# One pair of PSUM banks for the running sum, two pairs for the state, in a chunked selective-scan block

## The reference, cut to what matters

```python
def step(h, inp):                     # one chunk of 128 tokens
    x_c, d_c, B_c, C_c = inp
    A_bar = jnp.exp(d_c[..., None] * A)
    BX = d_c[..., None] * B_c[:, :, None, :] * x_c[..., None]
    log_A_cum = jnp.cumsum(jnp.log(jnp.maximum(A_bar, EPS)), axis=1)
    A_cum = jnp.exp(jnp.minimum(log_A_cum, LOG_CLAMP))
    A_cum_sh = jnp.concatenate([jnp.ones_like(A_cum[:, :1]), A_cum[:, :-1]], axis=1)
    wcum = jnp.cumsum(BX / jnp.maximum(A_cum_sh, EPS), axis=1)
    h_chunk = A_cum * wcum / jnp.maximum(A_bar, EPS) + h[:, None] * A_cum
    y_c = jnp.einsum('bls,blds->bld', C_c, h_chunk) + D_param * x_c
    return (h_chunk[:, -1], y_c)
```

## Time and profile before

| | |
|---|---|
| time, median of 3 runs | 5796.58 us (5792.49 to 5797.22) |
| the profiled execution: its own time / its span | 5795.46 us / 5793.5 us |
| mean granted TensorE clock | 0.992 of full speed |
| PE busy | 5611.7 us (97%) |
| DVE busy | 5350.9 us (92%) |
| ACT busy | 3733.7 us (64%) |
| POOL busy | 2456.2 us (42%) |

### The profile page before, as it was taken

The page is one execution under the profiler, slowest core; times in us unless marked ns, Lnnn a source line. Parts: engine busy times, 40 slices in busy tenths (PEclk is TensorE's granted clock), DMA queues, the critical chain, the costliest instruction groups (busy, mean ns, idle before and its releaser), DMA issues. The chain is left out here.

```text
span 5793.5 us, 78230 instructions
## 1 busy us (share of the span) xinstructions
PE 5611.7 (97%) x16088; PEld 2641.4 (46%) x16152; DVE 5350.9 (92%) x7057; ACT 3733.7 (64%) x4615; POOL 2456.2 (42%) x2139
## 2 busy tenths in 40 slices
PE   8999999999999999999999999999999999999997
PEld 3444444444444444444444444444444444444443
DVE  7999999999999999999999999999999999999997
ACT  5666666666666666666666666666666666666664
POOL 3444444444444444444444444444444444444443
PEclk9999999999999999999999999999999999999999
DMA  2212212112121121121211212212112121121220
GB/s 69 19 16 16 20 14 18 16 15 20 14 18 18 16 18 16 15 20 14 18 17 15 20 14 17 20 14 18 16 15 20 14 18 17 17 18 16 15 18 12
DMA packets 158421, 104.23 MB, mean 18 GB/s; under 512 B 121024, under 2 KB 121024, under 8 KB 158016
## 3 DMA queue, kind: packets, MB, share of 16 engines
q1 hardware_dynamic: 158016, 100.71, 19.0%
HBM read 42.63 MB, written 16.78 MB: 10 GB/s over the span
## 5 line engine op out<-in xcount | busy, mean ns | idle before, releaser
L496 POOL TENSOR_SCALAR room<-total,limit 128x1024 f32<-128x1024 f32 x1024 | 1182.9, 1155 | 3244.6 <-PE cum L1068 475.1
L754 ACT ACTIVATE decay<-cum,neg_a 128x1024 f32<-128x1024 f32 x1024 | 1137.4, 1111 | 1539.2 <-PE cum L1068 1535.4
L1078 PE MATMUL state<-sources,tri_upto 128*128 128x512 f32 x4096 | 1971.8, 604 | 124.4 <-DVE term L1415 124.0
L1068 PE MATMUL cum<-step,tri_before 128*128 128x512 f32 x4096 | 1937.4, 595 | 0.1
L1415 DVE SCALAR_TENSOR_TENSOR term<-state,crow,decay 128x1024 f32<-128x1024 f32 x1024 | 1312.8, 1282 | 313.4 <-PE state L1078 197.1
L1425 DVE TENSOR_TENSOR acc<-acc,term 128x1024 f32<-128x1024 f32 x1024 | 1362.3, 1330 | 0.2
L1402 DVE SCALAR_TENSOR_TENSOR sources<-cum,brow,dx 128x1024 f32<-128x1024 f32 x1024 | 1305.8, 1275 | 7.2 <-ACT cum L770 7.2
L1068 PEld LDWEIGHTS cum<-step,tri_before 128*128 128x128 f32 x4096 | 780.1, 192 | 963.9 <-issue 939.2
L770 ACT ACTIVATE cum<-room,pos_a 128x1024 f32<-128x1024 f32 x1024 | 1143.5, 1117 | 108.9 <-POOL room L496 100.1
L1078 PEld LDWEIGHTS state<-sources,tri_upto 128*128 128x128 f32 x4096 | 742.5, 190 | 995.5 <-issue 867.8
L485 POOL TENSOR_SCALAR step<-delta,limit 128x1024 f32<-128x1024 f32 x1024 | 1144.5, 1118 | 42.7 <-DVE delta L1317 42.7
(11 more groups left out here) (127 smaller groups left out, 3626.3 us busy)
## 6 DMA issues: line engine op xcount, KB each, us to landing
hfirst<-hrows SPq DMA_DIRECT2D x496, 64.0 KB, 3.9
xt<-in_x SPq DMA_DIRECT2D x64, 256.0 KB, 2.6
hrows<-term SPq DMA_DIRECT2D x1024, 4.0 KB, 1.7
xres<-in_x SPq DMA_DIRECT2D x64, 256.0 KB, 2.6
out_x<-xres SPq DMA_DIRECT2D x64, 256.0 KB, 2.1
gate_last<-gate SPq DMA_DIRECT2D x512, 0.5 KB, 2.1
hrows<-hrows SPq DMA_DIRECT2D x64, 64.0 KB, 2.3
win<-in_w_in SPq DMA_DIRECT2D x2, 1024.0 KB, 7.9
```

What stands on the lines that cost most here:

```text
L496: nc.gpsimd.tensor_scalar(room[:, :], total[:, :], limit[:, s:s + 1], 0.0, ALU.min, ALU.max).then_inc(limited, 1)
L754: nc.scalar.activation(decay[s % 4][:, :], cum[s % 2][:, :], ACT.Exp, scale=neg_a[:, s:s + 1]).then_inc(decay_ready, 1)
L1068: last = nc.tensor.matmul(cum[s % 2][:, cols], tri_before[:, :], step[s % 2][:, cols], start=True, stop=True)
L1078: last = nc.tensor.matmul(state[:, cols], tri_upto[:, :], source[s % 2][:, cols], start=True, stop=True)
```

## The change

PSUM is dealt out anew: one pair of banks for `cum`, two pairs for `state`. `growths` writes its result into the `state` pair of the same slot instead of into `cum`; `states(s)` then overwrites it after `source(s)` has read it. With that, `states(s)` no longer waits for `term(s-1)`; `growths(s)` waits for `term(s-2)`, and `cumulate(s)` waits for `decays(s-1)`. `room` gets two buffers. The orders within slot s become:

- TensorE: `states(s)`, extras(s), `cumulate(s+2)`.
- ScalarE: some extras, `decays(s+1)`, `growths(s+1)`, the other extras.
- VectorE: `term(s-1)`, `add(s-1)`, extras(s), `source(s+1)`.
- GpSimd: `turn(s)`, `limit_step(s+2)`, `limit_sum(s+2)`.

Room for the second `room` buffer in SBUF comes from letting three small tiles share others (`ones` in `xnT[1]`, `csel` in `xi`, `qT` in `q_bf`). ScalarE's code path for `room` is removed; it had been used by no slot. The diff, cut to its core:

```diff
-        room = sb("room", [P, DI])
+        room = [sb(f"room{i}", [P, DI]) for i in range(2)]
...
+        qT = q_bf[:, :].rearrange("p (k t) -> p k t", t=P)
...
-        cum = [ps(f"cum{i}", [P, DI]) for i in range(2)]
-        state = ps("state", [P, DI])
+        cum = ps("cum", [P, DI])
+        state = [ps(f"state{i}", [P, DI]) for i in range(2)]
+        growth = state
...
             def limit_sum(t, s):
-                user, old = before(t, s, 1)
+                user, old = before(t, s, 2)
                 if user is not None:
                     pool.wait_ge(growth_ready, slot_at(user, old))
...
             def turn(t, s, more, more2):
...
                 else:
-                    pool.wait_ge(source_ready, slot_at(t, s))
+                    pool.wait_ge(added, slot_at(t, s - 2))
             def body(t, more, more2):                      # GpSimd
                 for s in range(NS):
                     turn(t, s, more, more2)
-                    if s + 2 < NS and s + 2 in ROOM_POOL:
+                    if s + 2 < NS:
+                        limit_step(t, s + 2)
                         limit_sum(t, s + 2)
...
-                    if s + 3 < NS:
-                        limit_step(t, s + 3)
...
             def end_q(t):                                  # ScalarE
...
+                if t.shift(-1) is not None:
+                    act.wait_ge(end_pe, at(END_PE, t.shift(-1), "ffn"))
                 nc.scalar.activation(q_bf[:, :], xn2, ACT.Identity, bias=round_back).then_inc(end_act, 1)
...
             def growths(t, s):
-                act.wait_ge(decay_ready, slot_at(t, s))
+                user, old = before(t, s, 2)
+                if user is not None:
+                    act.wait_ge(term_ready, slot_at(user, old))
+                act.wait_ge(limited, slot_at(t, s))
+                nc.scalar.activation(growth[s % 2][:, :], room[s % 2][:, :], ACT.Exp, scale=pos_a[:, s:s + 1]).then_inc(growth_ready, 1)
...
             def body(t, more, more2):                      # ScalarE
                 for s in range(NS):
-                    ahead, slot = (t, s + 2) if s + 2 < NS else (nxt, s + 2 - NS)
+                    ahead, slot = (t, s + 1) if s + 1 < NS else (nxt, 0)
...
                         decays(ahead, slot)
                     if s == 0 and prev is not None:
                         finish(prev)
+                    if more or s + 1 < NS:
+                        growths(ahead, slot)
                     if more:
                         if s == 0:
                             front_xi(nxt, 0)
...
-                    if more or s + 2 < NS:
-                        growths(ahead, slot)
...
             def cumulate(t, s):                            # TensorE
-                user, old = before(t, s, 2)
+                user, old = before(t, s, 1)
                 if user is not None:
-                    pe.wait_ge(source_ready, slot_at(user, old))
+                    pe.wait_ge(decay_ready, slot_at(user, old))
...
             def states(t, s):
                 pe.wait_ge(source_ready, slot_at(t, s))
-                user, old = before(t, s, 1)
-                if user is not None:
-                    pe.wait_ge(term_ready, slot_at(user, old))
...
             def body(t, more, more2):                      # TensorE
                 for s in range(NS):
-                    if s + 2 < NS:
-                        cumulate(t, s + 2)
-                    elif more:
-                        cumulate(nxt, s + 2 - NS)
+                    states(t, s)
...
-                    states(t, s)
+                    if s + 2 < NS:
+                        cumulate(t, s + 2)
+                    elif more:
+                        cumulate(nxt, s + 2 - NS)
...
             def body(t, more, more2):                      # VectorE
                 for s in range(NS):
                         term_of(t, s - 1)
...
-                    if s + 1 < NS:
-                        source_of(t, s + 1)
-                    elif more:
-                        source_of(nxt, 0)
                     if s > 0:
                         add(t, s - 1)
...
+                    if s + 1 < NS:
+                        source_of(t, s + 1)
+                    elif more:
+                        source_of(nxt, 0)
```

More of the change, by code:

```diff
@@ L158, in mamba_block @@
         xnT = [sb(f"xnT{i}", [P, KD, P]) for i in range(2)]
+        ones = xnT[1][:, 0, :]
         xi = sb("xi", [P, DI])
@@ L214, in mamba_block @@
         abar = xcT[:, :, :].rearrange(flat)
+        csel = xi[0:NS, 0:P]
         rhs_sb = sources[:, :, :].rearrange("p a (b n) -> p (a b) n", n=D)
@@ L435, in _ @@
             nc.gpsimd.memset(flag[:, :], 0)
-            nc.gpsimd.memset(ones[:, :], 1.0)
+            nc.gpsimd.memset(ones, 1.0)
             nc.gpsimd.memset(ident[:, :], 0.0)
@@ L830, in body @@
                             front_square(nxt)
-                        if s == 15:
+                        if s == 14:
                             decay_once(nxt)
-                    if more or s + 2 < NS:
-                        if slot not in ROOM_POOL:
-                            rooms(ahead, slot)
+                    if more or s + 1 < NS:
                         decays(ahead, slot)
@@ L919, in consts_scale @@
                     pe.wait_ge(consts_dve, 6 + j)
-                    last = nc.tensor.matmul(ebank[:, j * P:(j + 1) * P], ones[:, :], rdiags[j], start=True, stop=True)
+                    last = nc.tensor.matmul(ebank[:, j * P:(j + 1) * P], ones, rdiags[j], start=True, stop=True)
                 last.then_inc(consts_pe, 1)
@@ L1019, in end_flag @@
                 end_free(t, "flag")
-                nc.tensor.matmul(ebank[0:1, 0:1], hm[:, 0:1], ones[:, 0:1], start=True, stop=True).then_inc(end_pe, 1)
+                nc.tensor.matmul(ebank[0:1, 0:1], hm[:, 0:1], tri_upto[:, P - 1:P], start=True, stop=True).then_inc(end_pe, 1)
             def end_yT(t, h):
@@ L1067, in cumulate @@
                     cols = slice(h * HALF, (h + 1) * HALF)
-                    last = nc.tensor.matmul(cum[s % 2][:, cols], tri_before[:, :], step[s % 2][:, cols], start=True, stop=True)
+                    last = nc.tensor.matmul(cum[:, cols], tri_before[:, :], step[s % 2][:, cols], start=True, stop=True)
                 last.then_inc(cum_ready, 1)
@@ L1072, in states @@
                 pe.wait_ge(source_ready, slot_at(t, s))
-                user, old = before(t, s, 1)
-                if user is not None:
-                    pe.wait_ge(term_ready, slot_at(user, old))
                 for h in range(2):
                     cols = slice(h * HALF, (h + 1) * HALF)
-                    last = nc.tensor.matmul(state[:, cols], tri_upto[:, :], source[s % 2][:, cols], start=True, stop=True)
+                    last = nc.tensor.matmul(state[s % 2][:, cols], tri_upto[:, :], source[s % 2][:, cols], start=True, stop=True)
                 last.then_inc(state_ready, 1)
@@ L1088, in finish @@
                         for cols in halves:
-                            last = nc.tensor.matmul(state[:, cols], tri_upto[:, :], carried[:, cols], start=True, stop=True)
+                            last = nc.tensor.matmul(carry_state[:, cols], tri_upto[:, :], carried[:, cols], start=True, stop=True)
                         last.then_inc(carry_sums, 1)
@@ L1093, in finish @@
                         for cols in halves:
-                            last = nc.tensor.matmul(state[:, cols], csel[:, :], hend[t.parity][:, cols], start=True, stop=True)
+                            last = nc.tensor.matmul(carry_state[:, cols], csel, hend[t.parity][:, cols], start=True, stop=True)
                         last.then_inc(carry_products, 1)
@@ L1121, in start @@
                 cumulate(t, 0)
-                cumulate(t, 1)
                 front_ct(t)
@@ L1125, in start @@
                 front_in(t.shift(1), "xi0", 0, 0)
+                cumulate(t, 1)
             def body(t, more, more2):
@@ L1413, in term_of @@
                     dve.wait_ge(carry_in, t.n + 1)
-                    done(nc.vector.tensor_tensor(state[:, :], state[:, :], abar, ALU.add), state_full, t.n + 1)
-                nc.vector.scalar_tensor_tensor(out=term[s % 2][:, :], in0=state[:, :], scalar=crow[t.parity][:, s:s + 1],
+                    done(nc.vector.tensor_tensor(state[s % 2][:, :], state[s % 2][:, :], abar, ALU.add), state_full, t.n + 1)
+                nc.vector.scalar_tensor_tensor(out=term[s % 2][:, :], in0=state[s % 2][:, :], scalar=crow[t.parity][:, s:s + 1],
                                                in1=decay[s % 4][:, :], op0=ALU.mult, op1=ALU.mult).then_inc(term_ready, 1)
```

59 lines of the change are left out of this document (20 added, 39 removed).

## The result

The median is 6091.36 us (6090.49 to 6091.97) against 5796.58: ratio 1.051, 95% interval 1.0487 to 1.0534. The change makes the kernel 295 us slower. The forecast had the direction, but with 145 us only half of the size, and its range ended at 6060.

What follows compares the result with a forecast made beforehand. TensorE and VectorE were taken as nearly level bounds. TensorE's 86.2 us of work plus 5.63 of standing gave 91.8 a tile against 89.54, 145 us more over 63 tiles: 5940 us, range 5770 to 6060.

Steps and rivals of the forecast that it cites:

- the loop's turn: Slot 0 after the loop's jump: some 1.95 us of VectorE idle left, TensorE stands 1.6 every second tile, 0.8 a tile.
- The 86.2: TensorE's own work in us a tile, from 89.54 less its waits; 87.1 at most.
- the 0.9 taken off for the weight load's wait and the small ones: Waits for ScalarE's `xcT` and in the quantized product, taken to delay TensorE's matmuls 0.9 us a tile, between 0 and 0.97.
- `add` starts 1.38 after `term`: VectorE, each slot: `add` directly follows `term` and needs its result, so starts 1.39 us after it, not 1.20.
- the sources of slots 5 and 15: Sign of being right: TensorE's `states` waits for `source` there in every tile, 1.3 to 1.6 us each.
- `end_h` waits for `end_hT`: Slot 3: VectorE waits for TensorE's result, which sets its lead to zero; TensorE then stands 1.63 us in slot 4.
- neither `decay` nor `step`: `cumulate`'s waits for ScalarE's `decay` and GpSimd's `step`, costed at nothing; uncovered, `step` would cost 1.1 us a slot.
- `growths(9)`: Slots 7 to 12: behind ScalarE's table loads, VectorE loses what it gains; cost to TensorE near 0.
- VectorE's share: Sign of being right: VectorE's busy share, 92% before, rises.
- the 0.19: Extra us VectorE pays in each slot for `add` right behind `term`, 3.04 a tile; bounds 0 and 0.19.
- the faster rival: VectorE keeps a lead and TensorE's waits go; VectorE's floor of 87.6 us a tile gives 5680 us; chance 0.17.
- The clock rival: Stands bring TensorE's lower clock, at most 1.7 us lost a tile: 6047 us; chance 0.09.

Runs made afterwards that it cites:

- without fetch and branch: The carries' untaken branch left out on all engines, code where it was: changed kernel 5942.29 us, kernel before 5794.70 us.
- the moved after: The changed kernel with 80 more semaphore increments at the head of TensorE's program, so its loop begins elsewhere in the packets: 6006.26 us.
- the late branch: VectorE's carries' branch moved behind `source(1)`, against the padded changed kernel with the carries' sums in the running sum's banks (6008.18 us): 5958.94 us.
- late adds: VectorE's `add` of each slot but the first put behind that slot's other work, against the padded changed kernel (6006.26 us): 6203.26 us.

## Why the prediction was wrong

The step that failed is a mis-sized term, the loop's turn, with 1.6 us every second tile and bounds of 0 and 3.16. Measured, the tile with the turn takes 97.59 - 91.05 = 6.54 more. The term counted VectorE's jump alone. That part was right: without fetch and branch the two tiles are 1.64 apart (92.56 and 90.92). It left out TensorE's code fetch, 3.12 for two tiles (188.64 - 185.52), and the untaken branch, 2.04 (185.52 - 183.48), which the prediction names only as one that "no row shows taken" and gives no price. Here the untaken branch holds VectorE up by 0.89 us at the turn (2.03 - 1.14), and the change put `source(1)` behind it. (The prediction also reckons with 31 turns; the loop jumps back 28 times.)

The sum, with its 0.8 a tile for the turn, gave 145 us, and the kernels without fetch and branch differ by 147.6. That is partly luck: the stands came out smaller (3.28 against 4.83), TensorE's own time larger, 87.8 against 86.2. The 86.2 was too low already for the kernel before: its tiles less all of TensorE's idle time, away from the lower clock, take 87.0 to 87.1, the forecast's upper bound, so the 0.9 taken off for the weight load's wait and the small ones was not there. The other 0.7 came with the change.

Point by point: `add` starts 1.38 after `term`, as said. `states` waits 1.37 and 1.09 for the sources of slots 5 and 15. `end_h` waits for `end_hT`, 119.7 / 64 = 1.9 us a tile. `cumulate` stood 1.2 us in the whole run, so it waited for neither `decay` nor `step`. VectorE stands 1.7 us a tile for `growths(9)`, but no stand of TensorE came of it. VectorE's share was to rise and fell, 92% to 88%: its busy time rose by 26 us only, and the span by 295; 0.10 of the 0.19 is idle (1.38 less the 1.28 that `term` is busy). TensorE's share fell to 93%, near the 94 forecast. That VectorE has to wait in `end_h` is shown, and that undoing it gives 33 us; whether a lead without the collision would have brought the faster rival, no run shows. The clock rival did not come in its size: the mean granted clock was 0.990 after and 0.992 before, and by the tiles with and without the lower level (97.8 to 99.9 and 96.6 us after, 89.5 and 88.0 before) it cost some 29 us after and 19 before, an estimate.

## What to carry to other kernels

Read the instruction queues' lines of both pages before explaining a stand "issue" or one of an engine's own sequencer: an edit that only adds or drops waits can move a loop so that its code no longer stays loaded (85 us here), and a few idle instructions ahead of the loop undo it. Ask what runs just before each jump and branch, taken or not, and keep what the bound engine waits for ahead of it. A dependent operation right behind its producer may be the cover for the next one's input: look for what that one waits for before moving it away. And after moving work, compare the durations of single operations, not only the waits: an `add` or a tap that meets GpSimd's work shows as busy, two to three times as long, and no list of waits names it.

## What the runs showed of the hardware

A stand of 2.2 us at the turn was followed by a lower clock, as in the earlier trace rows: windows of the moved after (length, busy time of PE, PEld, DVE, ACT, POOL, then PEclk, DMA share, GB/s), up to the turn's end and just behind it.

```profile
984.00:988.19 4.19, 1.97 (x5) 0.68 (x4) 3.89 (x4) 3.04 (x4) 2.21 (x2) 1.00 0.32 80
988.19:991.60 3.41, 3.41 (x5) 1.34 (x4) 3.31 (x3) 1.12 (x1) 0.79 (x1) 0.50 0.01 1
```

TensorE had stood 2.22 us before it, and 0.50 is the level of 1.2 GHz. This came behind 9 of the 28 turns of that run, and behind none with the late branch, where the stand was 1.34 us in the turn read. So the 0.9 us that the late branch takes from VectorE's path were worth more than themselves: 49 us where 28 x 0.89 make 25. The nine tiles with the lower clock took 95.6 us against 93.8, 16 us of the rest.

The `add` and the taps, whose two inputs both lie in SBUF, and GpSimd's operations held each other up wherever they met for more than 0.2 us: the `add` ended 1.08 us behind `skip` in each of four kernels, two taps took 1.1 us in place of 0.35 beside `limit_step` and `limit_sum`, and with late adds `limit_step` itself took 1.84 us as its median in place of 1.11. `term` and `source`, one input of which lies in PSUM, kept their 1.27 to 1.28 us beside the same operations.
